# Attention scores from head pairs stacked through DRAM instead of block-diagonal halves, in a one-core decoder layer

## The reference, cut to what matters

```python
# self attention: B=32, S=112, H=16, Hd=16
scores = jnp.einsum('bqhd,bkhd->bhqk', Q, K) * scale
scores = scores + _alibi_bias(S, H, x.dtype)[None]
attn = jax.nn.softmax(scores, axis=-1)
out = jnp.einsum('bhqk,bkhd->bqhd', attn, V).reshape(B, S, D) @ Wo + bo
# cross attention: 375 keys
sm = jnp.einsum('nlhd,nshd->nlhs', q, k) / math.sqrt(D)
sm = jax.nn.softmax(sm, axis=1)
attn = jnp.einsum('nlhs,nshd->nlhd', sm, v).reshape(N, L, H * D) @ Wo + bo
# layer
x = _layernorm(x + self_attention(x))
x = _layernorm(x + cross_attention(x, ctx, ctx))
x = _layernorm(x + quantised_ffn(x))
```

## Time and profile before

| | before |
|---|---|
| median of 3 runs | 1259.4 us (1258.11 to 1260.34) |
| the profiled execution: device time, span | 1256.11 us, 1254.3 us |
| TensorE busy in the span | 1137.2 us (91%) |
| VectorE busy | 1070.1 us (85%) |
| ScalarE busy | 934.0 us (74%) |
| GpSimd busy | 448.1 us (36%) |

### The profile page before, as it was taken

The page is one execution under the profiler, slowest core; times in us unless marked ns, Lnnn a source line. Parts: engine busy times, 40 slices in busy tenths (PEclk is TensorE's granted clock), DMA queues, the critical chain, the costliest instruction groups (busy, mean ns, idle before and its releaser), DMA issues. The chain is left out here.

```text
span 1254.3 us, 28844 instructions
## 1 busy us (share of the span) xinstructions
PE 1137.2 (91%) x8658; PEld 843.2 (67%) x8658; DVE 1070.1 (85%) x2303; ACT 934.0 (74%) x3155; POOL 448.1 (36%) x463
## 2 busy tenths in 40 slices
PE   1589999999999999999999999999975998989498
PEld 1456666666667666766666766666543988778498
DVE  6259999999999999999999999999874559989698
ACT  1368888888888888888888888888742569855595
POOL 0223334433334433333433333443110007767343
PEclk9899999999999999999999999999986999999799
DMA  5000000000100000100000100010000000000133
GB/s 165 23 17 27 28 22 21 21 21 23 34 22 20 20 20 20 34 24 20 20 20 20 30 29 20 20 33 22 5 4 8 1 1 0 1 1 1 32 104 99
DMA packets 35059, 32.85 MB, mean 26 GB/s; under 512 B 4164, under 2 KB 34748, under 8 KB 35004
## 3 DMA queue, kind: packets, MB, share of 16 engines
q1 hardware_dynamic: 32704, 31.50, 8.4%
q10 hardware_dynamic: 2300, 0.66, 0.3%
HBM read 24.81 MB, written 7.34 MB: 26 GB/s over the span
## 5 line engine op out<-in xcount | busy, mean ns | idle before, releaser
L593 ACT ACTIVATE Px<-score 125x896 f32<-125x896 f32 x128 | 117.4, 917 | 89.4 <-PE score L1121 89.4
L574 ACT ACTIVATE Ps<-score,nmax_s 112x112 f32<-112x112 f32 x512 | 176.3, 427 | 4.0 <-DVE nmax_s L797 4.0
L585 ACT ACTIVATE Px<-score,nmax_h 125x112 f32<-125x112 f32 x512 | 172.6, 367 | 0.8 <-DVE nmax_h L790 0.8
L790 DVE TENSOR_REDUCE nmax_c<-score 125x8 f32<-125x896 f32 x128 | 136.2, 1064 | 13.6 <-PE score L1040 10.4
L574 ACT ACTIVATION_READ_ACCUMULATOR Ps<-score,nmax_s 112x1 f32 x512 | 144.3, 282 | 0.0
L759 DVE TENSOR_REDUCE Zc<-Px 125x8 f32<-125x896 f32 x128 | 137.9, 1077 | 5.7 <-ACT Px L593 2.1
L504 POOL TENSOR_TENSOR Kbd_hi<-Ks_hi,mask 128x448 fp32r<-128x448 f32 x64 | 63.9, 999 | 202.9 <-PE score L1040 137.5
L1132 PE MATMUL outX<-Px,Vn 125*32 125x224 f32 x1536 | 113.6, 368 | 7.2 <-DVE Vn L773 7.2
L585 ACT ACTIVATION_READ_ACCUMULATOR Px<-score,nmax_h 125x1 f32 x512 | 113.0, 221 | 0.0
L525 POOL TENSOR_TENSOR rstd<-vare,half 112x1 f32<-112x1 f32 x64 | 35.1, 548 | 177.0 <-DVE vare L882 177.0
L531 POOL TENSOR_TENSOR xb<-x_in,abo 112x256 f32<-112x256 f32 x32 | 23.7, 739 | 200.2 <-DVE r L868 200.2
(11 more groups left out here) (244 smaller groups left out, 3638.2 us busy)
## 6 DMA issues: line engine op xcount, KB each, us to landing
ctx_in<-in_ctx SPq DMA_DIRECT2D x32, 375.0 KB
x_in<-in_x SPq DMA_DIRECT2D x32, 112.0 KB, 2.0
x_scratch<-x SPq DMA_DIRECT2D x32, 112.0 KB, 1.9
x2T_all<-x_scratch SPq DMA_DIRECT2D x32, 112.0 KB, 2.1
out<-x2T_all SPq DMA_DIRECT2D x32, 112.0 KB, 1.9
raw_w_up<-in_w_up SPq DMA_DIRECT2D x1, 768.0 KB, 5.6
raw_w_down<-in_w_down SPq DMA_DIRECT2D x1, 768.0 KB, 7.4
raw_w_gate<-in_w_gate SPq DMA_DIRECT2D x1, 768.0 KB, 9.5
```

Source lines behind the costliest of these rows:

```text
L574: ins = act.activation(Ps[:, g, :], score[slot][0:L, h // QUAD, (h % QUAD) * L:(h % QUAD + 1) * L], ACT.Exp, bias=nmax_s[:, g:g + 1], accu ...
L585: ins = act.activation(Px[u % 2][:, h, :], score[SLOT_OF[f"C{u}"]][0:C, h // QUAD, (h % QUAD) * L:(h % QUAD + 1) * L], ACT.Exp, bias=maxim ...
L593: act.activation(Px[u % 2][:].rearrange("s (q h) l -> s q (h l)", q=2), score[SLOT_OF[f"C{u}"]][0:C, :, 0:QW], ACT.Exp).then_inc(exp_c, 1)
L790: dve.tensor_reduce(dst, score[SLOT_OF[f"C{u}"]][0:C, :, 0:QW].rearrange("s q (h l) -> s q h l", h=QUAD), AX.X, ALU.max, negate=True).then ...
```

## The change

Scores are made by head pairs. The three products of hi and lo parts become one product over 96 stacked rows: 32 rows of a pair's keys three times as (hi, lo, hi), against the pair's queries as (hi, hi, lo). One operand of each pair is laid on a block diagonal of two heads, so one product has 2 x 112 = 224 columns and covers the whole array; 4 of them make a unit. In self attention six rows with the ALiBi terms stand below the 96. The stacks are laid by transfers: the hi and lo parts go from SBUF to a DRAM scratch and come back into the rows where they are needed: per batch 5 transfers out (`Ks`, `Qs`, `Qx` with 128 rows of 1792 bytes each, the two halves of `Kx` with 128 x 2 rows of 1500 bytes), and 21 back (6 for `Ks` and 6 for `Qx` of 57 KB, 3 for `Qs` of 115 KB, 2 x 3 for `Kx` of 192 KB); 26 transfers with 3.64 MB in all. All are issued by SyncE, beside the three of before, which move 0.6 MB per batch.

Beside that: the maxima of the cross units go straight into `shift`, as the moving operand of a product with an identity (`unit`), without the transpose and the copy; GpSimd no longer masks, but adds the two halves of the exponentials ahead of VectorE's sum, and normalises the self probabilities, so spread, transpose and multiplication behind them are gone; `norm` is written as another instruction; there is a third `work` bank and a third buffer of `Px`; there are eight stages, and each engine's list has a new order.

```diff
-STAGES = 7
+STAGES = 8
-        KxT = [[sb(f"KxT{q}_{p}", [P, KT, S], F32R) for p in ("hi", "lo")] for q in range(2)]
+        KxS = sb("KxS", [STACK, PAIRS, S], F32R)
+        QxS = sb("QxS", [STACK, 2, QUAD, KT, L], F32R)
+        QsS = sb("QsS", [STACK + ALIBI, QUAD, KT, L], F32R)
+        KsS = sb("KsS", [STACK + ALIBI, 2, QUAD, KT, L], F32R)
-        work = [ctx.enter_context(nc.psum_tensor(f"work{p}", [P, BANK], F32)) for p in range(2)]
+        work = [ctx.enter_context(nc.psum_tensor(f"work{p}", [P, BANK], F32)) for p in range(3)]
...
+            def lay_on_diagonal(n, name, stack, parts, laid):
+
+                for i, part in enumerate(parts):
+                    rows_ = stacks_dram[name][n.par, :, part].rearrange("(j e r) k l -> e r j (k l)", e=2, r=HD)
+                    for e in range(2):
+                        at = PAIR_ROWS * i + HD * e
+                        sp.dma_start(stack[at:at + HD, e].rearrange("r j k l -> r j (k l)").bitcast(F32), rows_[e])\
+                            .then_inc(laid, 16)
...
+            def lay_queries_cross(n):
+                saved, read = counts(n.times(16, 16), n.times(NU))
+                sp.wait_ge(qx_saved, saved)
+                wait(sp, scores_c, read)
+                lay_on_diagonal(n, "Qx", QxS, PARTS_OF_Q, qx_laid)
...
+                pool.tensor_tensor(Ph[p][:], Px[u % NPX][:, :, 0:L // 2], Px[u % NPX][:, :, L // 2:L], ALU.add)\
+                    .then_inc(halved_c, 1)
...
             def cross_scores(n, u):
                 t, c = divmod(u, NC)
                 wait_slot(n, f"C{u}")
-                if c == 0:
-                    wait_drain(pe, (n, f"K{t}"))
-                    pe.wait_ge(qbd_done, n.times(KT, t + 1))
-                row_halves(score[SLOT_OF[f"C{u}"]][0:C], KxT[n.par], Qbd, t, slice(c * C, (c + 1) * C), True)\
-                    .then_inc(scores_c, 1)
+                pe.wait_ge(kx_laid[t], n.times(16 * 3, 16 * 3))
+                pe.wait_ge(qx_laid, n.times(16 * 6, 16 * 6))
+                for j in range(HALF):
+                    q, at = j // 2, j % 2 * 2 * L
+                    ins = pe.matmul(score[SLOT_OF[f"C{u}"]][0:C, q, at:at + 2 * L].rearrange("s (e l) -> s e l", e=2),
+                                    KxS[:, HALF * t + j, c * C:(c + 1) * C], QxS[:, :, j, t, :],
+                                    start=(at == 0), stop=True, skip_group_check=True)
+                ins.then_inc(scores_c, 1)
...
+                    ins = pe.matmul(score[SLOT_OF[f"C{u}"]][0:C, q, 0:QW], unit[:],
+                                    maxima.rearrange("s (h o) -> s h o", o=1).broadcast_to([C, QUAD, L]),
                                     start=False, stop=True, skip_group_check=True)
```

More of the change, by code:

```diff
@@ L224, in load_rows @@
                 .then_inc(self.const_ld, 16)
[L225 to L242, removed]
+        eng.dma_start(self.even_odd[:], self.a["even_odd"]).then_inc(self.const_ld, 16)
+        eng.dma_start(self.alibi_l, self.a["alibi_l"]).then_inc(self.const_ld, 16)
+        eng.dma_start(self.alibi_r, self.a["alibi_r"]).then_inc(self.const_ld, 16)
 def quantise_weights(nc, a, ident, wT, w_down, constants):
@@ L477, in save_x2, with counts, save_parts @@
                     .then_inc(x2_saved, 16)
-            def step(n0, n1, n2, n3, n4, n5, n6):
-                if n3:
-                    load_ctx(n3)
+            def counts(*values):
+                return [v if isinstance(v, int) else sp.to_reg(v) for v in values]
+            def save_parts(n, use, parts, saved):
+                wait_drain(sp, (n, use))
+                sp.dma_start(stacks_dram[use][n.par].rearrange("p c k l -> p (c k l)"),
+                             parts[:].bitcast(F32).rearrange("p c k l -> p (c k l)")).then_inc(saved, 16)
@@ new lines, in lay_keys_self, with lay_queries_self @@
+            def lay_keys_self(n):
+                saved, read = counts(n.times(16, 16), n.times(KT))
+                sp.wait_ge(ks_saved, saved)
+                wait(sp, scores_s, read)
+                lay_on_diagonal(n, "Ks", KsS, PARTS_OF_K, ks_laid)
+            def lay_queries_self(n):
+                saved, read = counts(n.times(16, 16), n.times(KT))
+                sp.wait_ge(qs_saved, saved)
+                wait(sp, scores_s, read)
+                lay_side_by_side(n, "Qs", QsS, PARTS_OF_Q, qs_laid)
@@ new lines, in lay_keys_cross @@
+            def lay_keys_cross(n, t):
+                saved, read = counts(n.times(16, 16), n.back(1).times(NU, NC * (t + 1)))
+                sp.wait_ge(kx_saved[t], saved)
+                wait(sp, scores_c, read)
+                for i, part in enumerate(PARTS_OF_K):
+                    sp.dma_start(KxS[PAIR_ROWS * i:PAIR_ROWS * (i + 1), QUAD * t:QUAD * (t + 1), :].bitcast(F32),
+                                 stacks_dram["Kx"][n.par, part, t * P:(t + 1) * P]
+                                 .rearrange("(j r) s -> r j s", r=PAIR_ROWS)).then_inc(kx_laid[t], 16)
@@ L651, in even_self @@
                 wait_fill(act, (n, use))
-                wait(act, sum_s, n.back(1).times(KT, t + 1))
+                wait_drain(act, (n.back(1), use))
                 act.activation(evenT[:, t, :], work[WORK_OF[use]][:, 0:L], ACT.Copy,
@@ L1033, in three @@
                 return pe.matmul(dst, lhs[1], rhs[0], start=False, stop=last)
-            def row_halves(dst, lhs, rhs, t, cols, first):
-                for i, (a, b) in enumerate(((0, 0), (0, 1), (1, 0))):
-                    for q in range(2):
-                        rows = slice(HALF_ROWS * q, HALF_ROWS * (q + 1))
-                        ins = pe.matmul(dst[:, q, 0:QW], lhs[a][rows, t, cols],
-                                        rhs[b][rows, t].rearrange("p h l -> p (h l)"),
-                                        start=(first and i == 0), stop=(i == 2))
-                return ins
             def transpose_rows(n, use, src):
@@ L1164, in transpose_probs @@
                 b = fill(n, use)
[L1165 removed]
+                pe.wait_ge(probs_s, n.times(KT, j // 2 + 1))
                 for h in range(QUAD):
```

670 lines of the change are left out of this document (331 added, 339 removed), and 3 rows, old and new, of the table WORK_USES.

## The result

The changed kernel takes 1172.37 us in the median of 4 runs (1170.62 to 1173.13), against 1258.76 of the kernel before in the same comparison (1257.91 to 1260.34): a ratio of 0.931, 95% interval 0.9294 to 0.9327. The forecast was 1205 us, range 1165 to 1285: the direction held and the time lies in the range, but 86 us came off where 54 were forecast, and 1172 us lies just outside the 1178 to 1240 us that the prediction gave as the own range of its forecast. The profiled execution took 1172.56 us with a span of 1170.7.

The account below looks back on a forecast made before the run. TensorE was taken to bound the loop; 2.24 us less per step over 31 steps saves 69 us, the eighth stage adds 15: 1256 - 69 + 15 = 1202, plus 3.3 for the median, 1205 us, range 1165 to 1285.

Parts of the forecast that it names:

- TensorE bounds the kernel before: Loop of the kernel before: TensorE 26.6 us of a 27.0 us step, idle 0.4, VectorE next at 25.1.
- Score products at 0.105 us: TensorE's 32 new 224-column products at 0.105 us each; six cross units save 1.14 us, two self halves 0.82 per step.
- the first rival: Narrow score products run at plain fp32 rate, 0.415 us instead of 0.105: 1513 us; chance 0.15.
- Transposes and shift: TensorE, per step: transposes of maxima and reciprocals save 0.80 + 0.36 us; four shifts at 0.52 cost 0.88 more.
- The rest of TensorE's list, costed at nothing: TensorE's units that the change leaves alone: no saving counted in the 2.24 us per step.
- The third bank at nothing: Third work bank: costed at nothing; could give back TensorE's idle 0.4 us, or take about as much if its order is worse.
- VectorE stays below 21.9: VectorE per step: shorter sums save 1.9 us and two spreads of 0.676 go, leaving at most 21.9 us.
- the fourth rival: More comes off than counted, with VectorE or ScalarE near 22 us coming close: step 23.5 us, 1165 us; chance 0.07.
- Transfers: SyncE's 29 transfers, 4.24 MB per step, stay hidden at 59% load; QxS is covered with 3 us to spare.
- The second rival: Stacks come late through SyncE's ordered list, 1 to 3 us of stall per step: 1236 to 1298 us; chance 0.17.
- The third: Rival: fixed part of 26 transfers not overlapped, 1.9 us each, 49 us per step: 1950 us; chance 0.01.
- The eighth stage: One partly filled step added ahead of the first store: 15 us, bounds 0 and 24.8.

Follow-up runs that it names:

- the last run: Kernel before, with the six products of each cross unit issued twice: 1357.12 us, ratio 1.0777.
- the doubled runs: Cross units' products issued twice, in the kernel before (1357.12 us) and in the changed kernel with values 4 and 5 normalised earlier (1191.96 us).
- the run with the values ahead and doubled products: Changed kernel with VectorE's products of values 4 and 5 ahead of the self reciprocals, and cross units' four products issued twice: 1191.96 us, ratio 0.9468.
- the maxima's run: Kernel before, with maxima straight into shift, without their transposes and copies, order and half-height scores kept: 1273.55 us, ratio 1.0116.
- the runs on the kernel before: Kernel before with maxima straight into shift: 1273.55 us; the same with a third work bank: 1256.52 us.
- the run with two banks: Changed kernel with uses spread over two work banks, self values in two buffers and copied earlier on ScalarE: 1544.21 us, ratio 1.2266.
- the fastest version: Changed kernel with VectorE's products of values 4 and 5 moved earlier and that of values 0 moved later: 1129.92 us, ratio 0.8974.
- the run with the context first: Changed kernel with SyncE's context load issued ahead of the six transfers of QxS: 1214.79 us, ratio 0.9652.

## Why the prediction was right or wrong, step by step

**TensorE bounds the kernel before.** Right: the list of 26.6 us is confirmed by the last run.

**Score products at 0.105 us.** Right. The starts lie 0.105 to 0.111 apart, a unit takes 0.51 to 0.52, and the first rival (0.415) is out. Summed over the starts in the doubled runs, less what was doubled, scores went from 6.3 to 4.2 us per step: 2.1 off, 1.96 forecast.

**Transposes and shift.** The transposes gave 1.0 (forecast 1.16). `shift` was mis-sized: in the run with the values ahead and doubled products, where TensorE is never idle, its four take 1.70 us, where 4 x 0.52 = 2.08 were forecast, and 1.31 stood before: 0.4 dearer, not 0.88. The 0.10 for a change of work that I added to each isn't there.

**The rest of TensorE's list, costed at nothing: the step that failed most.** All units that the change doesn't touch went from 18.0 us (30.28 less 8.13 for doubled cross units, 1.88 self, 1.31 `shift`, 1.00 transposes) to 15.9 us per step (24.32 less 5.72, 1.02 and 1.70), summed from the starts of the same two runs: 2.1 us that I hadn't counted. With 2.1 + 1.0 - 0.4 = 2.7 from the priced items that is the 4.8. No such product became faster in itself (one of `aWq` has 0.112 to the next in both); the starts differ where one unit follows another. In these two runs 1.65 of the 2.1 us lie at the last products of the untouched units, from their start to that of the next unit (5.40 us per step, now 3.75), and the rest within units, where first products differ (that of `aWq` had 0.20 to the second behind a self half, and has 0.10 now). The whole step has 37 changes of unit instead of 46, and cheap ones are new: the last product of `aWo` has 0.03 to a score unit instead of 0.31 to `outX`, of which that unit's first product gives back some 0.1 (0.62 at 402.46 for 0.51). A last score product has 0.11 to the next unit instead of 0.29 or 0.30 out of a pair of half height, as the rows of the maxima's run show; this part is in the scores' 2.1 above. How much is due to the full height and how much to the new order of neighbours wasn't separated; the runs on the kernel before say only that neither direct maxima nor a third bank brings it in the old order.

**The third bank at nothing.** Nearly right for the old order (0.4 us per step, beside direct maxima). In the new order it can't be judged by itself, as the run with two banks shows.

**VectorE stays below 21.9.** Wrong: 22.7. The sums shrank as estimated (609 ns for 0.6), the spreads are gone, but the products of `Vn` lost 1.8 us per step beside GpSimd's new instructions: 22.7 - 1.8 = 20.9, and 421.38 us of 450 in the fastest version are 21.0 per step. I had looked at whether GpSimd had time, not at what its work does to VectorE's. So the bound did not stay with TensorE: its list fell by 4.8 us, but the step now holds 2.0 us of waits in round trips with VectorE (23.8 against 21.8) where it held 0.4, so 3.2 us arrived; moving three products gave 1.4 back. This is nearest to the fourth rival (step 23.5, 1165), with its reason half right: more came off, and VectorE came close, by another price.

**Transfers.** Hidden, as forecast, and no wait of TensorE names one. But the cover is thinner than the 3 us I worked out. SyncE's issues in the timeline, first those ahead of the six transfers and then the six, and their row on the page (KB each, median us to landing):

```profile
416.33 1.25 SPq L493 DMA_DIRECT2D QsS<-Qs_parts  x3
417.84 0.34 SPq L463 DMA_DIRECT2D x_scratch<-x  x1
418.38 1.27 SPq L523 DMA_DIRECT2D KxS<-Kx_parts  x3
419.83 2.65 SPq L503 DMA_DIRECT2D QxS<-Qx_parts  x6
```

```profile
QxS<-Qx_parts SPq DMA_DIRECT2D x192, 56.0 KB, 3.2
```

2.65 and 3.2 stand for 6 x 0.34 and 1.9 of the forecast; these six had all landed at 424.6, 1.7 us ahead of the cross unit at 426.3 (1.0 to 2.1 in other steps of the loop). The chain had also left something out: the six don't start behind the last cross unit, which ran from 416.57 to 417.09, but 2.7 us later, when SyncE has issued what stands ahead of them in its list. That 1.7 us were left all the same is due to the window between the two units, 9.2 us where 7 were forecast. The DMA share is 0.68 for the forecast 59%, 179 GB/s. The second rival is a true mechanism, as the run with the context first shows, 1.7 us from deciding. The third is out: 26 transfers go in 23.8 us, so their fixed part overlaps. The rule of the Trainium skill, "DMA: Bandwidth & Descriptors", section "Rules for kernel authors", that transfers under 64 KB pay mostly overhead, agrees with a landing of 3.2 us for 56 KB, which at the loop's 179 GB/s are 0.3 us of bytes, but not as a price per transfer here.

**The eighth stage.** 26.4 us later for the first store, where 15 were taken, beyond even the upper bound of one step. The stretch ahead of the first store of x2 in the kernel before:

```profile
30.00:149.00 119.00, 99.91 (x718) 69.43 (x718) 78.47 (x179) 78.69 (x319) 38.03 (x51) 0.94 0.07 20
```

TensorE is idle in 35 of 146 us now, in 19 of 119 then: 16 of the added 27 us are waiting. And the clock of 0.91 for 0.94 means, with 1.2 GHz as half of 2.4, 2 x 0.09 x 146 = 26 us at the lower level instead of 2 x 0.06 x 119 = 14. No run tells these apart. At the other end the last eight steps take 145.8 us instead of 185.3, 4.9 us less each, about as much as TensorE's list fell by. That would fit a VectorE with less to do there (122.81 of 146 us), but the units of the first stages are missing in these steps, over eight stages instead of seven, so it isn't shown.

**The sum, by what was measured:** first store 26.4 later instead of 15, and 31 steps 3.57 shorter instead of 2.24: 110.7 instead of 69. That the time lies in the range at all is in part luck: TensorE's list fell by 4.8 us where 2.24 were priced, and the step got less of it only because VectorE, which was taken to stay out of the way, held it up. With three products moved the same change takes 1129.92 us, below the range.

## What to carry to other kernels

Price a new list by its neighbours too: the units that the change left alone take 2.1 us per step less, most of it where one follows another, as much as the score products that the change was about gave. When an engine gets new work beside the bound, ask what its instructions do to those of the engine it runs beside, and place the work where the other reads PSUM or is idle. A busy share of 95% doesn't say who sets the step: doubling a known piece does, for the price of one run.

## What the runs showed of the hardware

VectorE's product of two SBUF operands (125x128, fp32) takes 0.28 us when GpSimd has nothing, and up to 1.25 us in the loop beside GpSimd's product of 112x896; it ends 0.14 us behind it. VectorE's maximum over 896 scores in PSUM takes 1.04 us beside it and 1.05 alone. With three of the six products per step moved away the longest of all is 344 ns instead of 2336. The Trainium skill, "SBUF — State Buffer", section "Who interferes with whom", says that a VectorE instruction with two SBUF inputs contends with a GpSimd instruction that reads SBUF, and that one then blocks until the other ends. The trace agrees with both, and the prediction hadn't weighed it. The trace of the kernel before shows it too, beside one of GpSimd's masks; such a product takes 0.49 us there and ends 0.15 us behind the mask:

```profile
408.23 0.49 DVE L773 TENSOR_TENSOR Vn<-Vx,rZc 125x128 f32<-125x128 f32 x1
```

```profile
407.64 0.93 POOL L504 TENSOR_TENSOR Qbd_lo<-Qx_lo,mask 128x448 fp32r<-128x448 f32 x1
```

A pair of score products of half height takes 0.20 us ahead of its like and 0.29 to 0.30 ahead of a product of full height; a product of 96 rows takes 0.105 to 0.111, whether its like or a product of full height follows. The Trainium skill, "TensorEngine Tiling (Array Packing)", section "Key Properties", says that a change of tiling mode drains TensorE; these 0.09 us agree with that, though no run here varies the mode alone.
